# Shared expert with its weights stationary: gate and up products turned, inner values written to PSUM

## Chip, cores and metric

The kernel runs on one core of a Trainium2 chip. The metric is device time of one execution in microseconds, the lower the better; several executions give a median.

## What is computed

Sixteen sequences of 128 tokens with 256 features pass through a pre-norm decoder layer: causal attention with 16 heads and rotary positions, a long convolution gated by a context tensor, and a feed-forward part with 16 routed experts (4 per token) and one shared expert. The change touches the shared expert alone:

```python
x = x + attn(layernorm(x)); x = x + conv_mix(layernorm(x), ctx)
h = layernorm(x)                                   # 2048 tokens x 256
gate, up = split(h @ shared_gate_up.T, 704)        # shared_gate_up: 1408 x 256
shared = (silu(gate) * up) @ shared_down.T         # 704 -> 256
shared = shared * sigmoid(h @ shared_gate_vec.T)
out = x + shared + sum_of_routed_experts(h)
```

Products are made of fp16 pairs: every fp32 operand is a high and a low half, and a product is high x high, high x low and low x high, three matmuls. Silu is computed with a tanh: silu(g) = g/2 (1 + tanh(g/2)).

## The kernel before, in words

Work runs in two phases. In the first, one *row* (one sequence of 128 tokens) enters per *stage*, and the pieces of several rows are interleaved; in the second, 79 tiles of 128 sorted tokens pass through the routed experts. Each engine has a list of pieces (`ORDER`), written out by hand, which it goes through once per stage; `name:behind` means that in stage s the piece works on row s - behind. Every engine runs its list strictly in order and waits at semaphores. Stages 0 to 4 fill the pipeline, stages 5 to 16 hold every piece, and a second written list (`DRAIN`) finishes rows 12 to 15 and what is left of the others. Names of pieces that the text uses:

- TensorE: `px` prefix sums for routing (lines 689 to 694); `ga0`, `ga1`, `up0`, `up1` gate and up of the shared expert, each for 352 of the 704 inner values (`half_product`, line 705); `v` and `qk` projections (528); `sc01`, `sc23` scores (568, 574); `pt0` to `pt3` transposes of probabilities (585); `at0` to `at3` attention times values (597); `cv0` to `cv3` quarters of the convolution (632, 636); `Th0`, `Th1` transposes of the inner values (`turn_shared`, 715); `t5` transpose for the feed-forward (660); `dn` the shared down product (727); `Tq`, `Tk` transposes of query and key terms (558).
- ScalarE: `th0`, `th1` tanh of the gates (1003); `hh0`, `hh1` high halves of the transposed inner values (1011); `ex0` to `ex3` exponentials (942, four instructions each); `ph0` to `ph3` copies of transposed probabilities (954); `kh2` the high half of a convolution operand (972); `cq`, `ck` copies of the transposed terms (923).
- VectorE: `s10`, `s11` (1 + tanh) x gate (1310); `s20`, `s21` times up, which gives the inner values (1320); `hl0`, `hl1` low halves (1327); `mx0` to `mx3` row maxima (1150); `pw` and `ky` routing steps (1285, 1295); `nr3` a normalisation shift (1113); `gm0` to `gm3` gating of the convolution (1206).
- GpSimd: `kl0` to `kl3` low halves of the convolution operands (1577).

Apart from these pieces ScalarE and VectorE also split the weights into halves, one *unit* after another as it is loaded. Where the units come in is set by the tables `PREPARE` (ScalarE) and `PREPARE_LO` (VectorE): `(stage, n): (units)` puts them ahead of the n-th piece of the list in that stage. VectorE's half of a unit is line 1347 or 1343.

PSUM has eight banks. `PSUM_ORDER` lists for each bank which pieces use it, in turn; before a piece writes, `free` waits until the reader of the use before has finished (table `READER`). In the kernel before, bank 0 is used by `up0`, `cv0`, `xT` (which `t5` writes) and `o2T` in turn, and `up0` counts as read when `s20` is done:

```python
"up0": (inner_done, 1), "up1": (inner_done, 2), "ih0": (inner_lo, 1), "ih1": (inner_lo, 2),
```

The operands of the convolution live in two buffers: `kh2` may only write when `cv0` has run, `kl2` follows `kh2`, and `cv2` needs `kl2`.

The shared expert of one row: tokens are the stationary operand and 352 weight columns move, so tokens lie on partitions; the inner values are computed in SBUF, transposed by TensorE (`Th0`, `Th1`) into PSUM, split into halves and multiplied by the down weights.

Of the kernel before, what the change touches and what calls it, by code (L numbers as in the profile page):

```python
# [1751 lines left out]
```

## Time and profile before

| what | us |
|---|---|
| median of three runs (608.62 to 612.01) | 611.7 |
| the profiled execution's own time | 609.71 |
| span of that execution in the profile | 607.9 |
| TensorE busy in the span | 575.1 (95%) |
| VectorE, ScalarE, GpSimd busy | 479.1, 413.0, 387.7 |

The span runs from the first to the last instruction of the profile; the execution's own time is 1.8 us longer. A busy TensorE counts matmuls from start to modelled end; matmuls overlap, so the time that one costs is read from the distance between starts.

### The profile page before, as it was taken

Reading aid. Unit: us, or ns where it says so; the run is one execution under the profiler, and the core shown is the slowest. Engines: PE = TensorE matmul, PEld = TensorE weight load, DVE = VectorE, ACT = ScalarE, POOL = GpSimd, SP = SyncE. Lnnn points to the kernel's source line nnn. Section 1 sums busy time; section 2 is a strip of 40 time slices with the busy share of each in tenths; the row PEclk is TensorE's granted clock in tenths of the full one; section 3 lists DMA queues with packets and bytes.
Section 4 is the critical chain, followed back from the end, with each engine's and each line's share of the span. In section 5 each row is a group of like instructions: output and inputs, shape, how many; then the busy total and the mean of one; then the engine's idle time right before and its main releaser. Section 6 shows DMA issues by size and latency. Waiting matters only on the chain.

```text
span 607.9 us, 18533 instructions
## 1 busy us (share of the span) xinstructions
PE 575.1 (95%) x5887; PEld 466.1 (77%) x5887; DVE 479.1 (79%) x1454; ACT 413.0 (68%) x1060; POOL 387.7 (64%) x419
## 2 busy tenths in 40 slices
PE   8889899999999999999999999998899999999991
PEld 3558679888898898888888889876677777777770
DVE  4657788878878688798877776687688899999993
ACT  4876876878768778787686775832266666666661
...
GB/s 227 295 80 174 92 111 122 80 132 116 92 135 79 114 115 62 148 83 129 90 87 86 14 87 24 32 45 63 146 128 135 175 222 237 235 238 233 243 179 112
DMA packets 55681, 78.99 MB, mean 130 GB/s; under 512 B 7202, under 2 KB 46370, under 8 KB 55588
## 3 DMA queue, kind: packets, MB, share of 16 engines
...
q8 instruction: 52, 0.85, 0.6%
...
HBM read 44.48 MB, written 33.29 MB: 128 GB/s over the span
## 4 chain that ended last, share of the span: by engine, by line
PE 78%; issue 7%; POOL 6%; DVE 4%; ACT 3%; DMA 1%; POOLq 0%; DVEq 0%; ACTq 0%
PE ps L832 12%; PE ps L705 9%; PE ps L597 7%; PE ps L632 6%; PE ps L528 5%; PE ps L727 5%; PE ps L855 4%; PE ps L652 3%; PE ps L585 3%; PE ps L636 3%; PE ps L844 3%; PE ps L821 3%; POOL kv_lo L1577 2%; PE ps L568 2%; PE ps L558 2%
## 5 line engine op out<-in xcount | busy, mean ns | idle before, releaser
L1577 POOL TENSOR_TENSOR kv_lo<-kv,kv_hi 128x512 f16<-128x512 f32 x64 | 80.9, 1265 | 30.2 <-ACT kv_hi L972 29.5
L1643 POOL DMA_INDIRECT toeplitz_lo<-y_slots,slots x44 | 42.5, 965 | 81.0 <-DMA y_slots<-kv 61.6
L832 PE MATMUL ps<-w_gate_up_hi,toeplitz_hi 128*128 x316 | 84.0, 314 | 1.4 <-DVE toeplitz_hi L1482 1.1
L1565 POOL TENSOR_TENSOR kv<-ctx_t_sb,v_t 128x512 f32<-128x512 f32 x60 | 64.9, 1090 | 16.0 <-ACT v_t L962 15.9
L1609 POOL DMA_INDIRECT x_slots<-x_norm,slots x60 | 65.0, 1084 | 15.1 <-issue 14.3
L942 ACT ACTIVATE probs<-ps,row_neg_max 128x128 f32<-128x128 f32 x256 | 71.5, 391 | 0.3 <-DVE row_neg_max L1150 0.3
L597 PEld LDWEIGHTS ps<-v_ones,probs_t 128*128 128x128 f32 x512 | 62.2, 192 | 2.2
L597 PE MATMUL ps<-v_ones,probs_t 128*128 128x17 f32 x512 | 60.7, 256 | 0.0
L1537 POOL TENSOR_TENSOR ln_rstd<-ln_var,minus_half 128x1 f32<-128x1 f32 x48 | 30.3, 632 | 43.1 <-DVE ln_var L1105 43.1
L632 PE MATMUL ps<-kv_hi,toeplitz_hi 128*128 128x128 f16 x256 | 56.7, 221 | 1.3 <-POOL kv_lo L1577 0.7
L632 PE MATMUL ps<-kv_hi,toeplitz_lo 128*128 128x128 f16 x256 | 56.6, 221 | 0.0
L1059 ACT ACTIVATE toeplitz_hi<-ps 128x256 f16<-128x256 f32 x79 | 30.2, 383 | 38.8 <-ACT stage L1078 17.4
L632 PE MATMUL ps<-kv_lo,toeplitz_hi 128*128 128x128 f16 x256 | 56.5, 221 | 0.0
L1206 DVE TENSOR_TENSOR conv_gated<-ps,ctx_t_sb 128x512 f32<-128x512 f32 x64 | 43.6, 684 | 12.4 <-PE ps L636 12.2
L636 PE MATMUL ps<-kv_lo,toeplitz_hi 128*128 128x64 f16 x256 | 49.7, 194 | 0.0
L636 PE MATMUL ps<-kv_hi,toeplitz_lo 128*128 128x64 f16 x256 | 49.7, 194 | 0.0
L636 PE MATMUL ps<-kv_hi,toeplitz_hi 128*128 128x64 f16 x256 | 49.7, 194 | 0.0
L832 PE MATMUL ps<-w_gate_up_lo,toeplitz_hi 128*128 x158 | 49.4, 313 | 0.0
L1150 DVE TENSOR_REDUCE row_neg_max<-ps 128x4 f32<-128x512 f32 x64 | 43.3, 682 | 7.6 <-PE ps L574 7.6
L972 ACT ACTIVATE kv_hi<-kv 128x512 f16<-128x512 f32 x64 | 40.1, 627 | 9.5 <-PE ps L636 8.5
L954 ACT ACTIVATE probs_t<-ps 128x512 f32<-128x512 f32 x64 | 38.7, 609 | 11.3 <-PE ps L585 10.7
L832 PEld LDWEIGHTS ps<-w_gate_up_hi,toeplitz_hi 128*128 128x128 f16 x316 | 30.7, 97 | 19.8 <-issue 9.4
...
## 6 DMA issues: line engine op xcount, KB each, us to landing
...
```

The source lines that it names most:

```text
L597: last = nc.tensor.matmul(bank("av")[:, h * (HD + 1):(h + 1) * (HD + 1)], pT[g % 2][:, s, :], v_sb[row % 2][:, h, :], start=True, stop=Tru ...
L632: nc.tensor.matmul(to, toep_w[a][:, QUADS * g + h, 0, :], kvh[b][g % 2][:, h, :, :].rearrange("p c n -> p (c n)"), start=first, stop=end, ...
L636: last = nc.tensor.matmul(to[:, 64:128], toep_w[a][:, QUADS * g + h, 1, :], kvh[b][g % 2][:, h, 0, :], start=first, stop=end, skip_group_c ...
L705: last = nc.tensor.matmul(bank(use, row)[:, 0:CH], xT[a][row % 2][:, kc, :], sgu[b][:, c, kc, side, :], start=first, stop=end)
L832: last = nc.tensor.matmul(psum[2 + t % 2][:, 0:2 * INTER], bxT[a][t % 2][:, kc, :], egu[b][:, bass.ds(e, 1), kc, :].rearrange("p a n -> p ...
L942: last = nc.scalar.activation(sm[g % 2][:, s, :], bank(f"sc{g}")[:, s * P:(s + 1) * P], ACT.Exp, bias=mx[row % 2][:, g, s:s + 1])
L1150: nc.vector.tensor_reduce(mx[row % 2][:, g, :], bank(f"sc{g}")[:].rearrange("p (s n) -> p s n", n=P), X, ALU.max, negate=True).then_inc(ma ...
L1206: nc.vector.tensor_tensor(to, y, cT.broadcast_to([P, QUADS, KC, SIDE, SIDE]), ALU.mult)\
L1565: nc.gpsimd.tensor_tensor(kv[g % 2][:], cs.broadcast_to([P, SIDE, SIDE, SIDE]), vs.broadcast_to([P, SIDE, SIDE, SIDE]), ALU.mult).then_inc ...
L1577: nc.gpsimd.tensor_tensor(flat(kvh[1][g % 2]), kv[g % 2][:].rearrange("p h j i -> p (h j i)"), flat(kvh[0][g % 2]), ALU.subtract).then_inc ...
L1609: pool.indirect_dma_start(out=xbuf, out_offset=bass.IndirectOffsetOnAxis(ap=slots[:, row, j:j + 1], axis=0), in_=xn3_of(row), in_offset=No ...
L1643: pool.indirect_dma_start(out=yg[n][j], out_offset=None, in_=ybuf[0:(last_tile(row, j) + 1) * P], in_offset=bass.IndirectOffsetOnAxis(ap=s ...
```

## The change

Gate and up change sides: 128 columns of weights are now stationary and the 128 tokens move, so that inner values come out on partitions and no transpose is needed. The 1408 columns are ordered as 384 gate, 384 up, 256 gate, 320 up and 64 gate, in 11 chunks of 128; the last chunk of `up1` holds 64 columns of up and 64 of gate, for which two pieces are new, `t1b` on ScalarE (a tanh of 64 x 128) and `s1b` on VectorE. `Th0`, `Th1` and the buffers `inner0`, `inner1` are gone: `s20` writes its product to the PSUM bank `ih0` and `s21` writes over `up1`, and `hh`, `hl` read them there. The shared gate's weight per token, which `s20` and `s21` applied, moves to the piece that adds the result to x. Banks are dealt anew, `pt1` stands ahead of `cv0` on TensorE, and `s20` stands behind `nr3` on VectorE. The tables of the weight units keep their stages and are renumbered.

```diff
 PSUM_ORDER = (
-    "up0:5 cv0:3 xT:4 o2T:3",
+    "up0:5 cv0:3 cv2:3 o2T:3",
...
-    "up1:5 cv2:3 xnT:0",
+    "up1:5 xnT:0",
...
-    "px:5 pt1:2 ih1:5 oT:2 wo:2",
+    "px:5 pt1:2 xT:4 oT:2 wo:2",
     "sc1:2 ih0:5 ro:4 tq:1",
...
-            "up1": (inner_done, 2), "ih0": (inner_lo, 1), "ih1": (inner_lo, 2), "dn": (xsh_ready, 1),
+            "up1": (inner_lo, 2), "ih0": (inner_lo, 1), "dn": (xsh_ready, 1),
...
-PREPARE_LO = {(2,9): (2,), (2,15): (3,), (2,30): (4,), (2,40): (5,), (3,30): (6,7), (3,42): (8,),
+PREPARE_LO = {(2,9): (2,), (2,15): (3,), (2,29): (4,), (2,41): (5,), (3,29): (6,7,), (3,43): (8,), (3,45): (9,),
...
-            def half_product(c, side, use, ready):
+            def half_product(use, first_col, chunks, ready):
...
-                    for kc in range(KC):
-                        for a, b, first, end in products(kc == 0, kc == KC - 1):
-                            last = nc.tensor.matmul(bank(use, row)[:, 0:CH], xT[a][row % 2][:, kc, :],
-                                                    sgu[b][:, c, kc, side, :], start=first, stop=end)
+                    for n in range(chunks):
+                        cols = slice(first_col + n * P, first_col + (n + 1) * P)
+                        for kc in range(KC):
+                            for a, b, first, end in products(kc == 0, kc == KC - 1):
+                                last = nc.tensor.matmul(bank(use, row)[:, n * P:(n + 1) * P], sgu[b][:, kc, cols],
+                                                        xT[a][row % 2][:, kc, :], start=first, stop=end,
+                                                        skip_group_check=True)
                     last.then_inc(ready.sem, 1)
-            def turn_shared(c):
...
+            pieces |= {"ga0": half_product("ga0", 0, 3, gate_ready), "up0": half_product("up0", 3 * P, 3, up_ready),
+                       "ga1": half_product("ga1", 6 * P, 2, gate_ready), "up1": half_product("up1", 8 * P, 3, up_ready)}
...
             def shared_up(c):
                 def piece(row):
-                    gate_done.wait(dve, row, c + 1)
+                    gate_done.wait(dve, row, 1 + 2 * c)
                     up_ready.wait(dve, row, c + 1)
-                    cws_done.wait(dve, row)
-                    inner_T.wait(dve, row - 1, c + 1)
-                    nc.vector.scalar_tensor_tensor(out=hh[c][:, 0:CH], in0=bank(f"up{c}", row)[:, 0:CH], scalar=cws[row % 2][:],
-                                                   in1=th[c][:], op0=ALU.mult, op1=ALU.mult).then_inc(inner_done.sem, 1)
+                    if c == 0:
+                        free(dve, "ih0", row)
+                    nc.vector.scalar_tensor_tensor(out=bank(("ih0", "up1")[c], row)[:, 0:CHP], in0=bank(f"up{c}", row)[:, 0:CHP],
+                                                   scalar=SILU, in1=th[c][:], op0=ALU.mult, op1=ALU.mult)\
+                        .then_inc(inner_done.sem, 1)
```

On TensorE, in a full stage, before: from the first probability transposes `pt0` over `cv0` to the attention `at0`. The last word of a row is what it waits for; `inner_done` is given by `s20` and `s21`.

```order
L585 MATMUL ps<-identity,probs 128x128 [waits exped]
...
L632 MATMUL ps<-kv_hi,toeplitz_hi 128x128 [waits inner_done,kv_lo]
...
L715 MATMUL ps<-identity,inner 128x128 [waits exped,inner_done]
...
L585 MATMUL ps<-identity,probs 128x128 [waits page_step,exped]
...
L597 MATMUL ps<-v_ones,probs_t 128x17 [waits x_shared_ready,v_copied,probs_t_copied]
...
L632 MATMUL ps<-kv_hi,toeplitz_hi 128x128 [waits probs_t_copied,kv_lo]
...
L632 MATMUL ps<-kv_hi,toeplitz_hi 128x128 [waits inner_done,kv_lo]
```

The same place now; `pt1` is the row that waits for `page_step`.

```order
L589 MATMUL ps<-identity,probs 128x128 [waits exped]
L589 MATMUL ps<-identity,probs 128x128 x3
L589 MATMUL ps<-identity,probs 128x128 [waits page_step,exped]
L589 MATMUL ps<-identity,probs 128x128 x3
L636 MATMUL ps<-kv_hi,toeplitz_hi 128x128 [waits inner_done,kv_lo]
...
L601 MATMUL ps<-v_ones,probs_t 128x17 [waits x_shared_ready,v_copied,probs_t_copied]
...
L636 MATMUL ps<-kv_hi,toeplitz_hi 128x128 [waits probs_t_copied,kv_lo]
...
L636 MATMUL ps<-kv_hi,toeplitz_hi 128x128 [waits conv_gated,kv_lo]
```

Between `cv0` and `cv2` (the first and the last convolution row) there stood `Th0`, `pt1`, `at0` and `cv1`; now `pt1` stands ahead of `cv0`, and only `at0` and `cv1` are left between the two.

On VectorE, in stage 6, before: from the second row maximum `mx1` to `s21`. `inner0` is written by `s20`, `inner1` by `s21`, the unit of weights is line 1347.

```order
L1150 TENSOR_REDUCE row_neg_max1<-ps5 128x4
L1280 TENSOR_TENSOR slot_place<-ps4,slot_moved 128x16
L1320 SCALAR_TENSOR_TENSOR inner0<-ps0,shared_weight0,gate_th0 128x352
L1347 SCALAR_TENSOR_TENSOR w_gate_up_lo<-stage,w_gate_up_hi 128x704
L1285 SCALAR_TENSOR_TENSOR tile_fresh<-ps4,tile_newest0 128x16
L1150 TENSOR_REDUCE row_neg_max1<-ps7 128x4
L1295 SCALAR_TENSOR_TENSOR slot_key<-picked0,slot_place 128x16
L1099 BN_AGGR ln_mean_var0_1<-ln_stats0_1 128x2
L1113 TENSOR_SCALAR ln_shift2_1<-ln_mean_var2_1,ln_rstd2_1 128x1
L1320 SCALAR_TENSOR_TENSOR inner1<-ps2,shared_weight0,gate_th1 128x352
```

The same place now; `s20` writes bank 5 from bank 0.

```order
L1154 TENSOR_REDUCE row_neg_max1<-ps5 128x4
L1284 TENSOR_TENSOR slot_place<-ps4,slot_moved 128x16
L1361 SCALAR_TENSOR_TENSOR w_gate_up_lo<-stage,w_gate_up_hi 128x704
L1289 SCALAR_TENSOR_TENSOR tile_fresh<-ps4,tile_newest0 128x16
L1154 TENSOR_REDUCE row_neg_max1<-ps7 128x4
L1299 SCALAR_TENSOR_TENSOR slot_key<-picked0,slot_place 128x16
L1103 BN_AGGR ln_mean_var0_1<-ln_stats0_1 128x2
L1117 TENSOR_SCALAR ln_shift2_1<-ln_mean_var2_1,ln_rstd2_1 128x1
L1332 SCALAR_TENSOR_TENSOR ps5<-ps0,gate_th0 128x384
L1154 TENSOR_REDUCE row_neg_max1<-ps1 128x4
```

`s20` stood ahead of the unit and stands now behind it, behind a row maximum and behind three short steps. In stages 5, 6, 7, 8, 10, 12 and 13 a unit stands somewhere between `mx1` and `nr3`; in the other full stages there is none there.

## Rows read from the trace of the kernel before

**Rows 1.** Page, first line: span.

```profile
span 607.9 us, 18533 instructions
```

**Rows 2.** Windows, one full stage: us, busy us by engine, clock, DMA share, GB/s.

```profile
320.03:344.48 24.45, 24.45 (x290) 20.93 (x289) 18.24 (x59) 18.32 (x45) 20.08 (x22) 1.00 0.19 61
```

**Rows 3.** Timeline of TensorE in stage 15: start us, length us, instructions.

```profile
331.66 0.31 PE L705 MATMUL ps<-w_shared_gate_up_hi,moe_x_t_hi 128*128 128x352 f16 x1
...
332.56 0.27 PE L528 MATMUL ps<-w_attn_hi,lhs_t_hi 128*128 128x256 f16 x1
...
333.40 0.59 PE L568 MATMUL ps<-causal_bf,identity_bf 128*128 128x512 bf16 x2
...
336.92 0.60 PE L585 MATMUL ps<-identity,probs 128*128 128x128 f32 x4
337.35 0.22 PE L632 MATMUL ps<-kv_hi,toeplitz_hi 128*128 128x128 f16 x1
...
337.52 0.19 PE L636 MATMUL ps<-kv_hi,toeplitz_hi 128*128 128x64 f16 x1
...
338.37 0.53 PE L715 MATMUL ps<-identity,inner 128*128 128x128 f32 x3
338.74 0.60 PE L585 MATMUL ps<-identity,probs 128*128 128x128 f32 x4
...
339.98 0.22 PE L632 MATMUL ps<-kv_hi,toeplitz_hi 128*128 128x128 f16 x1
...
341.00 0.22 PE L632 MATMUL ps<-kv_hi,toeplitz_hi 128*128 128x128 f16 x1
...
342.71 0.49 PE L715 MATMUL ps<-identity,inner 128*128 128x128 f32 x3
343.04 0.96 PE L597 MATMUL ps<-v_ones,probs_t 128*128 128x17 f32 x8
```

**Rows 4.** Timeline of ScalarE in the same stage; in brackets idle time before and who ended it.

```profile
331.04 1.02 ACT L923 ACTIVATE q_terms_t<-ps 128x1024 f16<-128x1024 f16 x1 [1.28 <-PE ps L558]
...
332.22 1.03 ACT L923 ACTIVATE k_terms_t<-ps 128x1024 f16<-128x1024 f16 x1
...
335.26 2.16 ACT L942 ACTIVATE probs<-ps,row_neg_max 128x128 f32<-128x128 f32 x8
...
338.63 0.63 ACT L972 ACTIVATE kv_hi<-kv 128x512 f16<-128x512 f32 x1 [0.48 <-PE ps L636]
...
341.03 0.62 ACT L954 ACTIVATE probs_t<-ps 128x512 f32<-128x512 f32 x1
```

**Rows 5.** Timeline of GpSimd in the same stage.

```profile
339.34 1.15 POOL L1577 TENSOR_TENSOR kv_lo<-kv,kv_hi 128x512 f16<-128x512 f32 x1 [0.85 <-ACT kv_hi L972]
```

**Rows 6.** Timeline of VectorE in stage 6, and TensorE's `cv0` there.

```profile
114.76 0.58 DVE L1320 SCALAR_TENSOR_TENSOR inner<-ps,shared_weight,gate_th 128x352 f32<-128x352 f32 x1
115.25 1.57 DVE L1347 SCALAR_TENSOR_TENSOR w_gate_up_lo<-stage,w_gate_up_hi 128x704 f16<-128x704 f32 x1
...
116.82 0.68 DVE L1150 TENSOR_REDUCE row_neg_max<-ps 128x4 f32<-128x512 f32 x1
...
117.98 0.57 DVE L1320 SCALAR_TENSOR_TENSOR inner<-ps,shared_weight,gate_th 128x352 f32<-128x352 f32 x1
...
116.13 0.22 PE L632 MATMUL ps<-kv_hi,toeplitz_hi 128*128 128x128 f16 x1
```

**Rows 7.** Timeline of VectorE: the units at that place in stages 5, 12 and 13.

```profile
91.47 0.93 DVE L1347 SCALAR_TENSOR_TENSOR w_gate_up_lo<-stage,w_gate_up_hi 128x704 f16<-128x704 f32 x1
...
263.44 2.15 DVE L1347 SCALAR_TENSOR_TENSOR w_down_lo<-stage,w_down_hi 128x1024 f16<-128x1024 f32 x1
...
287.83 2.22 DVE L1343 SCALAR_TENSOR_TENSOR w_down_rest<-stage,w_down_rest 64x1024 f16<-64x1024 f32 x1
```

**Rows 8.** Stage 4: timeline of TensorE (`pt0`) and ScalarE (`ex0` and `ex1`).

```profile
67.90 0.63 PE L585 MATMUL ps<-identity,probs 128*128 128x128 f32 x4 [0.92 <-ACT probs L942]
...
66.61 2.17 ACT L942 ACTIVATE probs<-ps,row_neg_max 128x128 f32<-128x128 f32 x8
```

More of the change, by code:

```diff
@@ L23 @@
 CH = SHARED // 2
+MIX = SHARED - 5 * P
 CHP = 3 * P
@@ L104 @@
 DRAIN = {n: [(p.split(":")[0], int(p.split(":")[1])) for p in pieces.split()] for n, pieces in {
[21 rows of a table removed]
[23 rows of a table added]
 }.items()}
 LATE_BANKS = (
-    "cv0:14 xT:13 o2T:14 cv0:15 xT:14 o2T:15 xT:15 up0:15",
+    "o2T:14 cv0:15 xT:14 o2T:15 xT:15 up0:15",
     "cv3:14 vT:15 cv3:15",
-    "cv2:14 cv2:15 ro:14 px:14 ro:15 px:15 up1:15",
+    "up1:12 cv2:15 ro:14 px:14 ro:15 px:15 up1:15",
     "",
-    "wo:15 px:13 up1:13 ih1:13 up1:14 ih1:14 ih1:15",
+    "wo:15 px:13 up1:13 up1:14",
     "ih0:12 ro:13 up0:13 ih0:13 up0:14 ih0:14 ih0:15",
@@ L239, in build @@
         seen = sb("seen", [P, NB + 1, EXPERTS], F16)
-        th = [sb(f"gate_th{c}", [P, CH]) for c in range(2)]
-        hh = [sb(f"inner{c}", [P, CHP]) for c in range(2)]
+        th = [sb(f"gate_th{c}", [P, CHP]) for c in range(2)]
         hT = [[sb(f"inner_t{c}_{n}", [P, 3, P], F16) for n in ("hi", "lo")] for c in range(2)]
@@ L380, in free @@
                 u, r = LATE_AFTER[use, row]
-                READER[u][0].wait(pe, r, READER[u][1])
+                if (u, r) != ("up0", row):
+                    READER[u][0].wait(pe, r, READER[u][1])
                 return
@@ L406, in unit_of @@
             if u < U_SD:
-                c, kc = divmod(u - U_SGU, KC)
-                return sgu[half][:, c, kc].rearrange("p s n -> p (s n)"), 2 * CH
+                kc, part = divmod(u - U_SGU, 2)
+                return sgu[half][:, kc, part * SHARED:(part + 1) * SHARED], SHARED
             if u < U_GU:
@@ L702, in piece @@
                     free(pe, use, row)
-                    for kc in range(KC):
-                        for a, b, first, end in products(kc == 0, kc == KC - 1):
-                            last = nc.tensor.matmul(bank(use, row)[:, 0:CH], xT[a][row % 2][:, kc, :],
-                                                    sgu[b][:, c, kc, side, :], start=first, stop=end)
-                    last.then_inc(ready.sem, 1)
-                return piece
-            def turn_shared(c):
-                def piece(row):
-                    inner_done.wait(pe, row, c + 1)
-                    free(pe, f"ih{c}", row)
-                    for t in range(3):
-                        last = nc.tensor.transpose(bank(f"ih{c}")[:, t * P:(t + 1) * P], hh[c][:, t * P:(t + 1) * P],
-                                                   id_sb[:])
-                    last.then_inc(inner_T.sem, 1)
+                    for n in range(chunks):
[5 more added lines that the diff above has]
+                                                        skip_group_check=True)
+                    last.then_inc(ready.sem, 1)
                 return piece
@@ L737, in _ @@
                 pieces |= {f"pt{g}": t_probs(g), f"at{g}": attend(g), f"cv{g}": conv(g)}
-            for c in range(2):
-                pieces |= {f"ga{c}": half_product(c, 0, f"ga{c}", gate_ready),
-                           f"up{c}": half_product(c, 1, f"up{c}", up_ready), f"Th{c}": turn_shared(c)}
+            pieces |= {"ga0": half_product("ga0", 0, 3, gate_ready), "up0": half_product("up0", 3 * P, 3, up_ready),
+                       "ga1": half_product("ga1", 6 * P, 2, gate_ready), "up1": half_product("up1", 8 * P, 3, up_ready)}
             def count_pairs():
@@ L789, in _ @@
                 pieces[name](row)
-                if (name, row) in table_after:
-                    table_after[name, row]()
+                for piece in table_after.get((name, row), ()):
+                    piece()
             def emptied(b):
@@ L1002, in piece, with rest_tanh @@
                     inner_done.wait(act, row - 1, c + 1)
-                    nc.scalar.activation(th[c][:], bank(f"ga{c}")[:, 0:CH], ACT.Tanh, scale=0.5 / WS)\
+                    n = (3 - c) * P
+                    nc.scalar.activation(th[c][:, 0:n], bank(f"ga{c}")[:, 0:n], ACT.Tanh, scale=0.5 / WS)\
                         .then_inc(tanh_done.sem, 1)
                 return piece
+            def rest_tanh(row):
+                up_ready.wait(act, row, 2)
+                inner_done.wait(act, row - 1, 2)
+                nc.scalar.activation(th[1][MIX:P, 2 * P:CHP], bank("up1", row)[MIX:P, 2 * P:CHP], ACT.Tanh, scale=0.5 / WS)\
+                    .then_inc(tanh_done.sem, 1)
             def inner_split(c):
                 def piece(row):
-                    inner_T.wait(act, row, c + 1)
+                    inner_done.wait(act, row, c + 1)
                     down_done.wait(act, row - 1)
-                    nc.scalar.activation(hT[c][0][:].rearrange("p t n -> p (t n)"), bank(f"ih{c}")[:, 0:CHP], ACT.Copy)\
+                    nc.scalar.activation(hT[c][0][:].rearrange("p t n -> p (t n)"), bank(("ih0", "up1")[c], row)[:, 0:CHP], ACT.Copy)\
                         .then_inc(inner_hi.sem, 1)
@@ L1037, in _ @@
                 pieces |= {f"th{c}": shared_tanh(c), f"hh{c}": inner_split(c)}
+            pieces["t1b"] = rest_tanh
             for s in range(DRAIN_FROM):
@@ L1326, in piece @@
                     inner_hi.wait(dve, row, c + 1)
-                    nc.vector.tensor_tensor(hT[c][1][:].rearrange("p t n -> p (t n)"), bank(f"ih{c}")[:, 0:CHP],
+                    nc.vector.tensor_tensor(hT[c][1][:].rearrange("p t n -> p (t n)"), bank(("ih0", "up1")[c], row)[:, 0:CHP],
                                             hT[c][0][:].rearrange("p t n -> p (t n)"), ALU.subtract)\
@@ L1335, in shared_out @@
                     dve.wait_ge(s_xsh[row % 2], 16 * (row // 2))
-                nc.vector.scalar_tensor_tensor(out=xsh[row % 2][:], in0=bank("dn")[:, 0:E], scalar=1.0 / WS,
+                cws_done.wait(dve, row)
+                nc.vector.scalar_tensor_tensor(out=xsh[row % 2][:], in0=bank("dn")[:, 0:E], scalar=cws[row % 3][:],
                                                in1=x2_of(row), op0=ALU.mult, op1=ALU.add).then_inc(xsh_ready.sem, 1)
@@ L1410, in _ @@
                 pieces |= {f"s1{c}": shared_gate(c), f"s2{c}": shared_up(c), f"hl{c}": inner_split(c)}
+            pieces["s1b"] = rest_gate
             for s in range(DRAIN_FROM):
@@ L1709, in weight_units @@
     units += [toep[:, q:q + QUADS] for q in range(0, GROUPS, QUADS)]
-    sgu = a["L0_ffn_shared_gate_up"].reshape(2, 2, CH, KC, P).transpose(1, 3, 4, 0, 2)
-    units += [sgu[c, kc] for c in range(2) for kc in range(KC)]
-    down = a["L0_ffn_shared_down"].T.reshape(2, CH, E)
-    down = np.concatenate([down, np.zeros((2, CHP - CH, E), np.float32)], axis=1)
+    gate, up = np.split(a["L0_ffn_shared_gate_up"], 2, axis=0)
+    n, m = CHP, SHARED - MIX
+    sgu = np.concatenate([gate[:n], up[:n], gate[n:m], up[n:m], up[m:], gate[m:]], axis=0).reshape(2 * SHARED, KC, P)
+    units += [w[:, n:n + SHARED] for w in sgu.transpose(1, 2, 0) for n in (0, SHARED)]
+    down = a["L0_ffn_shared_down"].T
+    down = np.concatenate([down, np.zeros((2 * CHP - SHARED, E), np.float32)], axis=0)
     units += list(down.reshape(2, 3, P, E).transpose(0, 2, 1, 3))
```

30 lines of the change are left out of this document (18 added, 12 removed), and 75 rows, old and new, of tables (DRAIN, ORDER, PREPARE, PREPARE_LO).

## The prediction

> **What bounds the kernel now.** I read the page's first part, then the windows for single stages, then TensorE's timeline through one stage, and last the other engines' timelines at the places where TensorE takes something over from them. The profiled span is 607.9 us [rows 1]. In a full stage TensorE is busy for 24.45 of 24.45 us at a granted clock of 1.00 (the 2.4 GHz level), while VectorE, ScalarE and GpSimd have about 6, 6 and 4 us to spare [rows 2]. So a full stage is as long as TensorE's list plus what TensorE waits for, and work taken from TensorE pays only where nothing else is late there. There are twelve full stages (5 to 16), half of the span; the routed tiles that follow are not touched.
>
> **TensorE's own work, per row.** Removed: four half products; `ga1` starts at 331.66 and the next piece at 332.56 [rows 3], so 0.90 us each for 6 matmuls, 3.60 in all. Removed also: `Th0`, 338.37 to 338.74, and `Th1`, 342.71 to 343.04 [rows 3], 0.70 together. Added: 11 chunks x 6 = 66 matmuls of 128 columns, each with weights of its own. The nearest row is the convolution, fp16, 128x128 weights, new ones for each matmul: three of them from 337.35 to 337.52 [rows 3], 0.057 each, so 66 x 0.057 = 3.76. From below, 128 columns at the rate of 352 columns per 0.15 us would be 0.0545 (3.60); from above, the four fp32 transposes from 336.92 to 337.35 [rows 3] give 0.108 (7.1). I take 0.057, the same shape and type. The net is 3.76 - 3.60 - 0.70 = -0.54 us per row, -8.6 over 16 rows if all of it came through. By piece: `ga0`, `up0`, `up1` (18 matmuls, 1.03) grow by 0.13 each, `ga1` (12, 0.68) shrinks by 0.22.
>
> The Trainium skill, "TensorE: Matmul & The Clock Gate", section "Back-to-back issue gap", speaks against small matmuls: in a stream of weight loads and matmuls it gives about 81 ns per matmul of 128 columns. The trace differs, with 57 ns for such pairs [rows 3]. By the Trainium skill's figure 66 matmuls would be an estimated 5.35 us, and each row 1.05 longer instead of 0.54 shorter.
>
> **What eats the saving in a plain stage.** Four waits, with each one's fixed length from the trace.
>
> (a) `sc01` starts at 333.40 [rows 3], after ScalarE's copies of the transposed terms: the first begins at 331.04, released by TensorE, and the second ends at 333.25 [rows 4]. That chain does not change, and `ga1` lies beside it. TensorE comes 0.22 earlier and waits 0.22 longer: gain nil. From here I count from `sc01`.
>
> (b) `up0` and `up1` push `pt0` from 336.92 to 337.18; `pt1`, which now stands ahead of `cv0`, takes another 0.43 (as long as `pt0` [rows 3]) and ends at 338.04. Its exponentials end at 337.42 [rows 4], so it does not wait. `cv0` needs `s20`, which now waits for the same exponentials (bank `ih0` follows `sc1`) and takes 0.58 x 384/352 = 0.63 [rows 6]: done at 338.05. The write to PSUM instead of SBUF is not shown by any row; I take 0, bounded by -0.1 and +0.3. So `cv0` starts at 338.05 to 338.1, a wait of at most 0.05, and ends at 339.1.
>
> (c) From the end of `cv0` (338.37, where `Th0` starts [rows 3]) `kh2` follows at 338.63 [rows 4] and `kl2` ends at 340.49 [rows 5]: 2.12, so about 2.15 until `cv2` can start. Between them stood 341.00 - 338.37 = 2.63 us of TensorE work; with `Th0` gone and `pt1` ahead of `cv0`, `at0` (0.81) and `cv1` (1.02) are left [rows 3], 1.83. TensorE waits 0.32. Behind `cv2` queue all later pieces of the stage.
>
> (d) `t5` now takes the bank of `pt1` and needs `ph1`, which ends at 341.03 + 0.62 [rows 4], 3.28 after the end of `cv0`; TensorE gets there after 2.15 + 1.02 = 3.17: 0.1.
>
> From `sc01` to the end of `pt3` that is +0.26 - 0.70 + 0.05 + 0.32 + 0.1 = +0.03, and `ga0` adds 0.13 later, ahead of nothing that could absorb it. A plain stage becomes 0.16 longer, x 12 = +1.9. The new `t1b` and `s1b` lie in spare time: ScalarE is idle 0.48 ahead of `kh2` [rows 4], VectorE has the 6 us of [rows 2].
>
> **What costs most: `s20` behind the weight units.** Both lists of VectorE are in the section on the change. In stages 5, 6, 7, 8, 10, 12 and 13 a unit's low half stands between `mx1` and `nr3`. It used to stand behind `s20`; now `s20` is behind it, and `cv0` waits for `s20`. In stage 6 `s20` started at 114.76, the unit at 115.25, `s21` at 117.98 [rows 6], so unit to `s21` is 2.73. The unit now starts at 114.76 and `s20` takes the place of `s21`: 117.49, done at 118.12. TensorE is ready for `cv0` at 116.13 [rows 6] plus 0.26 + 0.43 = 116.82. It waits about 1.3 us, and nothing later in the stage gives this back, since (c) and (d) run from the end of `cv0`, and (a) from the next `Tq`. For stages 7, 8 and 10, whose units have the same shape, I take the same. Stage 5 has a unit of 0.93 in place of 1.57 [rows 6, 7]: 0.7. Stages 12 and 13 have 2.15 and 2.22 [rows 7]: 1.9 each. Sum: 0.7 + 4 x 1.3 + 2 x 1.9 = +9.7. The low end is near 5, if units take 0.93 everywhere (0.7 x 5 + about 0.7 x 2); the high end 12, if the short steps behind the unit stretch too.
>
> **The filling and the draining.** In stages 3 and 4 there are no shared products between scores and `pt0`. In stage 4 `pt0` ran at 67.90, and `ex1` ends at 66.61 + 2.17 = 68.78 [rows 8]. `pt1` ahead of `cv0` therefore makes `cv0` start at 68.8 + 0.43 instead of 68.33, 0.9 later, and `kh2`, `kl2`, `cv2` follow. `pt1` no longer stands behind `cv0`, so I take 0.7 per stage (0 to 0.9), 1.4 for both. The drained rows 12 to 15 save at most 4 x 0.54 = 2.2; they get an extra VectorE step each where VectorE carries the routing chain. I take 0, with -2.2 and +2.
>
> **Sum.** +1.9 + 9.7 + 1.4 + 0 = +13.0. The profiled execution took 609.7, so 622.7; the runs shown (608.6 to 612.0, median 611.7) lie around 611, which gives 624.
>
> **Rivals.**
> 1. *TensorE's saving comes through* (faster). For it: TensorE is 100% busy in a full stage [rows 2]. Against it: (a) and (c) are chains whose length the change leaves, and the order of VectorE is as written. It needs `s20` on time in every stage and the waits (c) and (d) not there: 609.7 - 8.6 = 601 to 605.
> 2. *The two effects nearly cancel* (no change). The units run in about 0.9 us at their new place, so the stalls are near the low end of 5 us, and half of (c) is absorbed because ScalarE gets to `kh2` sooner (-2): 1.9 + 5 - 2 + 0.7 = +5.6, about 616. For it: stage 5 shows 0.93 [rows 7]. Against it: stage 6 shows 1.57 with GpSimd at work [rows 6].
> 3. *The new weights are not hidden* (much slower). Each matmul would step by more than 57 ns, at most by the 108 of the fp32 transposes: 66 x 0.051 = +3.4 us per row, +54, which with the stalls is above 660; a step of 0.08 gives 66 x 0.023 x 16 = +24, so 648. Against it: the convolution's 57 ns, and its 64-column matmuls go faster still (338.37 - 337.35 = 1.02 for 12 of each kind, so 0.028 each [rows 3]). The rule of the Trainium skill named above would be this rival.
>
> The three differ in sign at one point: how much later than TensorE `s20` is at `cv0`. With the plain stage as reckoned, an average stall of 0 gives about +3, 0.5 us in seven stages +7.
>
> **How the numbers follow.** Forecast 0.71, rival 1 0.11, rival 2 0.15, rival 3 0.03. About 1% is what a measurement of this kernel can tell from no change. Faster by over 1% (below 605.6): 0.11. Within 1%: rival 2 and the forecast's low edge, 0.17. Slower: 0.72. The forecast's own range is 618 to 630 (stalls of 5 to 12, PSUM write up to 0.3 in twelve stages, drain -2 to +2). The range for 8 in 10 must take in rival 2 and reaches down towards rival 1: 609 to 630.
>
> **What would show it.** Right: in stages 5 to 8, 10, 12 and 13 the first convolution matmul of `cv0` waits 0.7 to 2 us for VectorE's write of `ps`, and these stages last 25.3 to 26.6; the others last 24.6; `cv2` waits 0.3 for `kl2` in each; `sc01` waits 0.3; the new matmuls step by 0.057. Wrong: no wait at `cv0`, or stages of 24.0 us, would mean that VectorE is earlier than its order lets me think; a step over 0.06 would be rival 3; a longer tile phase would be a cause that I have not seen.

## The result and the profile after

The changed kernel takes 636.3 us (median of 6 executions, 631.7 to 639.8); the kernel before, run beside it, 610.9 (608.6 to 612.0). The ratio is 1.0425, 95% interval 1.0392 to 1.0458: slower, as forecast, but by 25 us where I had said 13, and above the range's end of 630. The profiled execution took 631.7 us, 22.0 more than that of the kernel before (609.7).

The page's first line and three windows of the changed kernel: stages 6, 12 and 15, as in [rows 2] (start and end; length; busy us of TensorE, its weight loads, VectorE, ScalarE, GpSimd; clock; DMA share; GB/s).

```profile
span 629.9 us, 19685 instructions
...
103.09:128.75 25.66, 24.92 (x328) 21.55 (x326) 20.41 (x61) 18.80 (x48) 20.45 (x22) 1.00 0.31 97
...
257.68:284.87 27.19, 24.93 (x325) 21.57 (x326) 22.70 (x63) 19.78 (x48) 19.91 (x22) 1.00 0.33 101
337.17:362.30 25.13, 24.84 (x328) 21.56 (x326) 19.79 (x60) 18.50 (x47) 20.17 (x22) 1.00 0.18 59
```

TensorE's list got shorter, but the plain stage 15 grew from 24.45 to 25.13 us: it now has 0.29 us of idle time, and its busy time grew as well (24.84). Stage 12 has 2.3 us of idle time. Stages are counted here from the start of one `qk` to the next; the *plain stage* is the length that the stages come back to where neither a weight unit nor the clock holds them up (stage 15 in the changed kernel). For every kernel of this study (the median of its executions; then us of the profiled execution, where "first `qk`" is that of stage 4 and "rest" is from the `qk` of stage 16 to the end of the span):

| kernel | median | first `qk` | plain stage | 12 full stages | rest |
|---|---|---|---|---|---|
| before | 610.9 | 75.3 | 24.45 | 293.5 | 239.1 |
| changed | 636.3 | 77.7 | 25.13 | 309.7 | 242.5 |
| e1_units | 622.1 | 77.6 | 25.13 | 301.9 | 241.1 |
| e2_rows | 632.9 | 77.4 | 24.87 | 311.4 | 241.7 |
| e3_pt1 | 632.0 | 76.1 | 25.13 | 309.8 | 242.3 |
| e4_before_pt1 | 618.2 | 79.2 | 24.55 | 297.8 | 240.5 |
| f1_three | 620.1 | 76.7 | 24.87 | 299.0 | 243.3 |
| f2p_psum | 623.7 | 78.4 | 24.88 | 300.3 | 246.0 |
| f2_sbuf | 613.4 | 78.4 | 24.39 | 292.9 | 244.6 |
| f3_all | 622.3 | 80.5 | 24.88 | 297.8 | 243.4 |
| f4_ph1 | 608.4 | 75.2 | 24.12 | 288.6 | 241.6 |
| f5_ck | 619.6 | 78.2 | 24.27 | 292.8 | 244.3 |
| b1_ck | 620.3 | 84.7 | 24.82 | 296.7 | 240.1 |
| b2_units | 609.0 | 74.0 | 24.45 | 292.4 | 240.6 |

The last three columns add up to the span of the profiled execution, which can lie some us from the median (`f2_sbuf`: 617.7 us where the median is 613.4). So the 22.0 us of the changed kernel are 2.4 in the filling, 16.2 in the twelve stages and 3.3 behind them. Of the 16.2, the plain stage's 0.68 x 12 is 8.2; the other 8.1 are stages longer than the plain one.

TensorE's waits (us in total, times, the longest):

```profile
PE ps L636 <- DVE ps L1332: 7.6, 7, 2.0
PE ps L589 <- ACT probs L938: 3.0, 6, 0.9
PE ps L664 <- ACT probs_t L950: 2.3, 13, 0.2
```

The first line is the forecast stall: `cv0` behind `s20`, in exactly seven stages, 7.6 us where I had 9.7; the kernel before has a single wait of that kind, of 0.2 us. The second line is `pt0` or `pt1` behind the exponentials (2.3 us in the kernel before). The third (`t5` behind `ph1`) is not in the list of the kernel before. The timeline of TensorE through stage 15, beside [rows 3]:

```profile
345.38 0.27 PE L724 MATMUL ps<-w_shared_down_hi,inner_t_lo 128*128 128x256 f16 x1
345.58 0.28 PE L724 MATMUL ps<-w_shared_down_hi,inner_t_hi 64*128 64x256 f16 x1
...
345.81 0.27 PE L724 MATMUL ps<-w_shared_down_hi,inner_t_lo 64*128 64x256 f16 x1
346.01 0.33 PE L652 MATMUL ps<-identity,skip_out 128*128 128x128 f32 x1
...
351.91 0.23 PE L711 MATMUL ps<-moe_x_t_hi,w_shared_gate_up_hi 128*128 128x128 f16 x1
351.97 0.22 PE L711 MATMUL ps<-moe_x_t_hi,w_shared_gate_up_lo 128*128 128x128 f16 x1
352.03 0.22 PE L711 MATMUL ps<-moe_x_t_lo,w_shared_gate_up_hi 128*128 128x128 f16 x1
...
354.80 1.04 PE L589 MATMUL ps<-identity,probs 128*128 128x128 f32 x8
355.76 0.22 PE L636 MATMUL ps<-kv_hi,toeplitz_hi 128*128 128x128 f16 x1
...
356.78 1.04 PE L601 MATMUL ps<-v_ones,probs_t 128*128 128x17 f32 x8
357.67 0.22 PE L636 MATMUL ps<-kv_hi,toeplitz_hi 128*128 128x128 f16 x1
...
358.66 0.19 PE L640 MATMUL ps<-kv_hi,toeplitz_lo 128*128 128x64 f16 x1
358.96 0.23 PE L636 MATMUL ps<-kv_hi,toeplitz_hi 128*128 128x128 f16 x1
...
359.96 0.19 PE L640 MATMUL ps<-kv_hi,toeplitz_lo 128*128 128x64 f16 x1
360.33 0.41 PE L664 MATMUL ps<-identity,x_norm 128*128 128x128 f32 x2 [0.18 <-ACT probs_t L950]
```

The new matmuls step by 0.06 and 0.055, as forecast. `cv2` starts 0.27 after `cv1` could hand over (358.66 + 0.03 to 358.96), `t5` 0.34 after `cv2`. And `dn` shows something that I had not counted: at its last chunk, whose weights have 64 rows, the step is 0.20 instead of 0.11, and again at the first matmul behind it.

What `cv2` and `t5` wait for, on ScalarE (`kh2`, `hh0`, `ph1`) and GpSimd (`kl2`), beside [rows 4, 5]:

```profile
357.04 0.63 ACT L968 ACTIVATE kv_hi<-kv 128x512 f16<-128x512 f32 x1 [0.70 <-PE ps L640]
...
359.20 0.50 ACT L1014 ACTIVATE inner_t_hi<-ps 128x384 f16<-128x384 f32 x1
359.57 0.62 ACT L950 ACTIVATE probs_t<-ps 128x512 f32<-128x512 f32 x1
```

```profile
357.75 1.16 POOL L1591 TENSOR_TENSOR kv_lo<-kv,kv_hi 128x512 f16<-128x512 f32 x1 [1.76 <-ACT kv_hi L968]
```

From the end of `cv0` (356.78) to `cv2` are 2.18 us; I had read 2.15 from the trace before.

VectorE in stages 6 and 12, unit and `s20`, beside [rows 6, 7]; then TensorE's `cv0` there:

```profile
119.56 0.88 DVE L1361 SCALAR_TENSOR_TENSOR w_gate_up_lo<-stage,w_gate_up_hi 128x704 f16<-128x704 f32 x1
...
121.51 0.55 DVE L1332 SCALAR_TENSOR_TENSOR ps<-ps,gate_th 128x384 f32<-128x384 f32 x1
...
275.44 2.15 DVE L1361 SCALAR_TENSOR_TENSOR w_down_lo<-stage,w_down_hi 128x1024 f16<-128x1024 f32 x1
...
277.64 0.55 DVE L1332 SCALAR_TENSOR_TENSOR ps<-ps,gate_th 128x384 f32<-128x384 f32 x1
```

```profile
122.21 0.22 PE L636 MATMUL ps<-kv_hi,toeplitz_hi 128*128 128x128 f16 x1 [0.45 <-DVE ps L1332]
...
278.33 0.22 PE L636 MATMUL ps<-kv_hi,toeplitz_hi 128*128 128x128 f16 x1 [1.97 <-DVE ps L1332]
```

The unit of stage 6 took 0.88 us at its new place, where 1.57 stood in [rows 6], and the stall is 0.45 where I had 1.3. Stage 12 came out as forecast (1.97 for 1.9).

Behind the stages, the chain of waits has its last `dn` at 453.96 in the changed kernel and at 435.33 in the kernel before (start, us):

```profile
453.96 3.56 PE ps L724 x18
```

```profile
435.33 2.14 PE ps L727 x18
```

From the last `qk` to there both took the same (66.54 and 66.56), so these two executions show no cost of the drain, as forecast. But TensorE's mean granted clock in that stretch was 1.00 in the changed kernel and 0.97 in the kernel before, so part of the equality is the clock's.

At the last `dn` itself it was the other way round. TensorE waited 1.0 to 1.1 us just ahead of it in both, and its mean granted clock over `dn` was 1.00 in the kernel before and 0.59 in the changed one, mostly the 1.2 GHz level; the window around it there:

```profile
453.00:458.00 5.00, 4.04 (x20) 2.38 (x21) 1.88 (x6) 0.00 (x0) 0.00 (x0) 0.66 0.39 110
```

So this `dn` took 1.4 us longer (about 0.2 of it are the 64 rows of the next section). The other 1.9 of the 3.3 lie in the routed tiles, which the change does not touch; their cause is open.

### The profile page after: what moved, and what is told of

Its sections match the earlier page's. It is cut to its first block, busy times and chain, and to the rows that moved or that the text cites. A ratio compares the mean times of both kernels' runs of the same rounds, so it can differ in the third digit from the quotient of the medians.

```text
span 629.9 us, 19685 instructions
## 1 busy us (share of the span) xinstructions
PE 579.9 (92%) x6463; PEld 476.2 (76%) x6463; DVE 493.4 (78%) x1468; ACT 416.5 (66%) x1076; POOL 387.3 (61%) x419
## 4 chain that ended last, share of the span: by engine, by line
PE 68%; issue 10%; ACT 7%; DVE 7%; POOL 4%; DMA 2%; POOLq 0%; ACTq 0%; DVEq 0%
PE ps L828 11%; PE ps L711 7%; PE ps L532 6%; PE ps L724 5%; PE ps L601 5%; PE ps L636 4%; PE ps L851 4%; PE ps L656 3%; PE ps L589 3%; PE ps L840 3%; ACT probs L938 2%; PE ps L817 2%; PE ps L640 2%; PE ps L572 2%; PE ps L562 2%
## 5 line engine op out<-in xcount | busy, mean ns | idle before, releaser
L1591 POOL TENSOR_TENSOR kv_lo<-kv,kv_hi 128x512 f16<-128x512 f32 x64 | 77.5, 1213 | 47.2 <-ACT kv_hi L968 47.1
L1579 POOL TENSOR_TENSOR kv<-ctx_t_sb,v_t 128x512 f32<-128x512 f32 x60 | 68.9, 1157 | 18.9 <-ACT v_t L958 18.8
L711 PE MATMUL ps<-moe_x_t_hi,w_shared_gate_up_hi 128*128 128x128 f16 x352 | 62.2, 220 | 2.1 <-DVE inner_t_lo L1340 2.1
L601 PE MATMUL ps<-v_ones,probs_t 128*128 128x17 f32 x512 | 62.2, 259 | 0.0
L711 PE MATMUL ps<-moe_x_t_lo,w_shared_gate_up_hi 128*128 128x128 f16 x352 | 62.0, 219 | 0.0
L711 PE MATMUL ps<-moe_x_t_hi,w_shared_gate_up_lo 128*128 128x128 f16 x352 | 62.0, 219 | 0.0
```

The costliest lines, as they stand in the source:

```text
L601: last = nc.tensor.matmul(bank("av")[:, h * (HD + 1):(h + 1) * (HD + 1)], pT[g % 2][:, s, :], v_sb[row % 2][:, h, :], start=True, stop=Tru ...
L711: last = nc.tensor.matmul(bank(use, row)[:, n * P:(n + 1) * P], sgu[b][:, kc, cols], xT[a][row % 2][:, kc, :], start=first, stop=end, skip ...
L1579: nc.gpsimd.tensor_tensor(kv[g % 2][:], cs.broadcast_to([P, SIDE, SIDE, SIDE]), vs.broadcast_to([P, SIDE, SIDE, SIDE]), ALU.mult).then_inc ...
L1591: nc.gpsimd.tensor_tensor(flat(kvh[1][g % 2]), kv[g % 2][:].rearrange("p h j i -> p (h j i)"), flat(kvh[0][g % 2]), ALU.subtract).then_inc ...
```

## The experiments

The diffs are shortened to the entries and lines that matter; "the changed kernel" is the one that the forecast was for.

**e1_units: the stalls of `cv0` alone.**

```diff
-(5,29): (14,) (6,27): (16,) (7,27): (18,) (8,27): (21,) (10,28): (25,) (12,31): (29,) (13,29): (32,)
+(5,34): (14,) (6,34): (16,) (7,34): (18,) (8,34): (21,) (10,34): (25,) (12,34): (29,) (13,34): (32,)
```

> The changed kernel with one edit: in stages 5, 6, 7, 8, 10, 12 and 13 the weight unit's low half that VectorE made ahead of s20 is made behind mx3, ahead of gm0. Theory 1 (the seven waits of cv0 for s20, 7.6 us in the trace, come from these units alone): the waits are gone, stages 6 to 13 last 25.1 to 25.4 us instead of 25.5 to 27.4, and the time falls by 6 to 8 us, to about 625 in the profiled execution. Rival (VectorE has too much to do in these stages, wherever the unit stands): gm0 then comes late, cv2 waits for its bank instead of cv0 for s20, and at most 3 us come back.

Measured: 622.1 us, ratio to before 1.0179 (1.0144 to 1.0215). The wait for `s20` is gone from the list, and the same two stages, 6 and 12, in its windows:

```profile
101.32:126.45 25.13, 24.84 (x327) 21.54 (x325) 20.57 (x61) 18.81 (x48) 19.86 (x22) 1.00 0.30 100
253.78:278.93 25.15, 24.86 (x326) 21.57 (x327) 21.53 (x63) 19.79 (x48) 19.93 (x22) 1.00 0.35 108
```

The twelve stages lose 7.8 us and the profiled execution 9.3, theory 1. Stages 9 and 11, which have units elsewhere in VectorE's list, are still long (25.65 and 25.99 us), outside the 25.1 to 25.4 of the text. The medians fall by 14, more than the waits were. The changed kernel's six executions run from 631.7 us at a mean granted clock of 0.988 to 639.8 at 0.972; those of e1_units from 621.0 to 622.9 at 0.986 to 0.992. So the stalls seem to cost clock as well; the next run's trace shows it in one execution.

**e2_rows: the 64 weight rows.**

```diff
-n = MIX if (c, t) == (1, 2) else P
+n = P
```

> The changed kernel with one edit: the last chunk of dn reads 128 rows instead of 64 (the added rows meet weights that are zero). Theory 2 (a change of the number of weight rows from 128 to 64 and back costs TensorE about 0.1 to 0.2 us each time): dn falls from 2.12 to about 1.9 us and the time by 0.2 to 0.25 us per row, 3 to 4 us over 16 rows. Rival (the time is that of dn's place, beside other work): dn stays at 2.1 and the time does not move by more than 1 us.

Measured: 632.9 us, 3.4 less, and 24.87 instead of 25.13 per plain stage: theory 2, 0.26 per row. The reading rests on the plain stage, since the executions of the two kernels overlap (630.2 to 633.6 and 631.7 to 639.8). The start of the last chunk of `dn` and the end of `dn` there:

```profile
322.36 0.27 PE L724 MATMUL ps<-w_shared_down_hi,inner_t_lo 128*128 128x256 f16 x1
322.46 0.27 PE L724 MATMUL ps<-w_shared_down_hi,inner_t_hi 128*128 128x256 f16 x1
...
322.68 0.27 PE L724 MATMUL ps<-w_shared_down_hi,inner_t_lo 128*128 128x256 f16 x1
322.79 0.27 PE L652 MATMUL ps<-identity,skip_out 128*128 128x128 f32 x1
```

Both steps of 0.20 are gone. The kernel before had chunks of 96 rows, which cost nothing (18 matmuls in 1.97 us). The Trainium skill, "TensorEngine Tiling (Array Packing)", section "Tiling Modes", states that a change of tiling mode drains TensorE; a row tile of 64 is such a mode there and 96 is none. The rows agree in what costs and what does not, with 0.1 us more at each of the two changes; that it is a drain, no row here shows. The kernel before may show the same price: its scores have 48 weight rows, and from the two matmuls of 512 columns and 128 rows ahead of them (333.40 [rows 3]) to the first of 48 rows (333.92) are 0.52 us, where two such steps in `qk` take 0.43. No run changes that place.

In this execution two stages were long, 27.9 and 29.5 us. Their windows, around the two stalls of 1.97 us, which ended at 277.13 and 305.01:

```profile
276.00:277.40 1.40, 0.27 (x7) 0.30 (x8) 1.40 (x4) 0.00 (x0) 0.00 (x0) 1.00 0.05 9
...
279.00:281.00 2.00, 2.00 (x27) 2.00 (x27) 1.94 (x5) 1.98 (x8) 1.89 (x2) 0.51 0.12 49
...
303.00:304.80 1.80, 0.05 (x1) 0.00 (x0) 1.77 (x6) 0.52 (x2) 1.17 (x1) 1.00 0.50 84
...
306.50:310.00 3.50, 3.50 (x38) 3.50 (x38) 2.69 (x7) 3.47 (x11) 3.00 (x4) 0.50 0.49 173
```

TensorE stood nearly idle in the first row of each pair; soon after its return, while it was fully busy, the granted clock was at 0.50, the 1.2 GHz level. The two stages are 1.0 and 2.6 us longer than those of the changed kernel less 0.26. The same stalls in the changed kernel's profiled execution left the clock at 1.00 in stage 12 (window above). So a stall of 2 us was followed, in this execution, by a further loss of half its length in one stage and 1.3 times its length in the next. That this is what made the other executions of the changed kernel 2 to 8 us longer than the profiled one is argued from their mean clocks, not seen in a trace of them.

**e3_pt1 and e4_before_pt1: the place of `pt1`.** In the changed kernel back behind `cv0`; in the kernel before ahead of it.

```diff
-pt0:2 pt1:2 cv0:3 at0:2
+pt0:2 cv0:3 pt1:2 at0:2
```

> The changed kernel with one edit: pt1 stands behind cv0 again in TensorE's list. Theory 3 (in a plain stage s20 holds cv0, so the cover that cv2 gets back is paid at cv0): cv0 waits 0.3 to 0.4 us for s20 in every stage, cv2 waits no more, plain stages stay within 0.1 of 25.13; the filling gives back 1.4 to 2.4; in sum 1 to 3 us less. Rival (pt1's place alone makes the waits of cv2 and t5): each plain stage is 0.4 to 0.6 shorter, and the time falls by 5 to 8 us.

```diff
-pt0:2 cv0:3 Th0:5 pt1:2 at0:2
+pt0:2 pt1:2 cv0:3 Th0:5 at0:2
```

> The kernel before with one edit: pt1 stands ahead of cv0 in TensorE's list. Theory 3 (with Th0 still there, 2.20 us of work cover the 2.18 from the end of cv0 to cv2): full stages stay at 24.45 to 24.55, the filling gets 1.4 to 2.4 us longer, in sum 1 to 3 us more than before. Rival (the place of pt1 is what lengthens the plain stages): 0.4 or more per stage, 5 us or more in sum.

e3_pt1: the plain stage stays at 25.13, and the wait is now at `cv0`:

```profile
354.20 0.22 PE L636 MATMUL ps<-kv_hi,toeplitz_hi 128*128 128x128 f16 x1 [0.36 <-DVE ps L1332]
```

The filling gives back 1.6. Theory 3: `s20` is what holds the stage, and the place of `pt1` only decides where TensorE waits for it. The time, 632.0 (628.5 to 636.5), fell by more than the 1 to 3 us of the text, but the twelve stages are unchanged (309.8 for 309.7).

e4_before_pt1 fell between the two: 618.2 us, 8 more than before, which is the rival's sum, not theory 3's 1 to 3. Plain stages are 24.55, as theory 3 had it, and the filling 3.9 longer instead of 1.4 to 2.4. But stages 6, 7 and 8 last 25.4 (and 9 and 11 25.3, which I did not trace). TensorE in stage 7 of this kernel, then VectorE:

```profile
145.15 0.60 PE L585 MATMUL ps<-identity,probs 128*128 128x128 f32 x4
146.50 0.63 PE L585 MATMUL ps<-identity,probs 128*128 128x128 f32 x4 [0.75 <-DVE tile_fresh L1285]
```

```profile
144.70 1.57 DVE L1347 SCALAR_TENSOR_TENSOR w_gate_up_lo<-stage,w_gate_up_hi 128x704 f16<-128x704 f32 x1
146.19 0.16 DVE L1285 SCALAR_TENSOR_TENSOR tile_fresh<-ps,tile_newest 128x16 f32<-128x16 f32 x1
```

`pt1` takes the bank that `pw` (`tile_fresh`) has read, and `pw` stands behind the unit. Neither theory had that bank. It is one reason why moving `pt1` forward is not free for the kernel before either; what lengthens the filling I did not trace.

**f1_three: the three edits together.** e1_units, e2_rows and e3_pt1.

> The changed kernel with the three edits of the first runs together: the seven weight units behind mx3, dn's last chunk with 128 rows, pt1 behind cv0. Theory (the three costs lie one behind the other on TensorE and add up): plain stages 24.87 us as with the 128 rows alone, stages 5 to 13 without stalls, first qk near 76.1; in sum 9 + 4 + 1.5 us less than the changed kernel's 631.7, about 617. Rival (they overlap): 620 or more.

Measured: 620.1 us (profiled 620.7), plain stage 24.87, twelve stages 299.0. In the stages the costs add up (-7.8 and 12 x -0.26 make -10.9; -10.7 measured). The sum of 617 was missed by 3.7, of which 2.1 are behind the last `qk`, compared with e1_units.

**f2p_psum and f2_sbuf: what makes `s20` late.** Both put `s20` ahead of `pw`; f2_sbuf also writes the inner values to SBUF.

```diff
-mx1:2 pp:5 pw:5 mx2:2 ky:5 ag1:0 nr3:4 s20:5 mx3:2
+mx1:2 pp:5 s20:5 pw:5 mx2:2 ky:5 ag1:0 nr3:4 mx3:2
```

> As the run with three edits, and s20 stands ahead of pw and mx2 in VectorE's list, as in the kernel before, still writing to PSUM. Theory (bank ih0 behind sc1 holds s20 until ex1 has ended, so its place in the list gives nothing): VectorE waits for ScalarE's exponentials at s20, cv0 still waits about 0.3, plain stages stay at 24.8 to 24.9, the time at that of the run with three edits. Rival (the place in the list held it): 24.4 to 24.5 per plain stage, 5 us less.

f2_sbuf, on top of it:

```diff
-free(dve, "ih0", row)
+inner_lo.wait(dve, row - 1, 1)
-out=bank(("ih0", "up1")[c], row)[:, 0:CHP]
+out=inner(c, row)
-"sc1:2 ih0:5 ro:4 tq:1"
+"sc1:2 ro:4 tq:1"
+hh = sb("inner0", [P, CHP])
+def inner(c, row): return bank("up1", row)[:, 0:CHP] if c else hh[:]
```

> As the run before it in this call, and s20 writes its inner values to a buffer in SBUF instead of bank ih0; the split reads them there. Theory (the bank, not VectorE's write, made s20 late): cv0 waits no more, cv2 stays covered by pt1, at0 and cv1 (2.26 for 2.18), plain stages 24.4 to 24.5, 4 to 5 us less than with PSUM, about 612. Rival (something else holds cv0 or cv2): 24.8 per plain stage and no gain.

f2p_psum: 24.88 per plain stage, nothing gained, and VectorE's timeline shows why; below it ScalarE's `ex0` and `ex1`:

```profile
346.61 0.57 DVE L1332 SCALAR_TENSOR_TENSOR ps<-ps,gate_th 128x384 f32<-128x384 f32 x1 [1.33 <-PE ps L711]
```

```profile
344.31 2.18 ACT L938 ACTIVATE probs<-ps,row_neg_max 128x128 f32<-128x128 f32 x8
```

VectorE stands still for 1.33 us. The bracket names TensorE, which had long delivered `up0`; `ex1` ends at 344.31 + 2.18 = 346.49, and `s20` starts right after. f2_sbuf: 24.39 per plain stage, 613.4 us, ratio 1.0043 (1.0021 to 1.0066). So with `s20` ahead of `pw`, the bank behind `sc1` costs 0.49 us per stage. The place in the list counts as well: in f1_three, where `s20` stands behind `nr3`, VectorE has no idle time ahead of it, and it starts at the same point of the stage as in f2p_psum (17.62 us after `qk` in both). Bank and place hold it equally late there, and only the two edits together set it free; SBUF at the late place was not run. The write itself costs nothing: 0.55 to 0.57 us to PSUM, 0.55 to SBUF.

**f3_all, f4_ph1, f5_ck: the remaining waits.** f3_all changes three things on top of f2_sbuf; f4_ph1 leaves `ck` and `vT` in their old order; f5_ck exchanges them after all, with another bank for `vT`.

```diff
-hh0:6 ph1:3 ex3:3
+ph1:3 hh0:6 ex3:3
-(9,38): (23,24,) (11,38): (27,28,)
+(9,41): (23,24,) (11,41): (27,28,)
-cq:2 vT:3 ck:2
+cq:2 ck:2 vT:3
```

> As the run with SBUF, and on ScalarE ck stands ahead of vT, ph1 ahead of hh0; the units of stages 9 and 11 stand behind gm1. Theory (sc01 waits 0.24 for ck and t5 0.2 to 0.3 for ph1 in each stage): both waits go, plain stages 23.9 to 24.1, stages 9 and 11 0.3 to 0.8 shorter, about 606, below the kernel before. Rival (TensorE then waits as long at the next of these chains, ex1, ph0 or cv2): 24.3 to 24.5, and no more than 1 us less than with SBUF alone.

```diff
-cq:2 ck:2 vT:3
+cq:2 vT:3 ck:2
```

> As the run with SBUF (s20 to a buffer in SBUF, ahead of pw; pt1 behind cv0; dn with 128 rows; units behind mx3), with ph1 ahead of hh0 on ScalarE and the units of stages 9 and 11 behind gm1, but ck and vT in their old order. Theory (the slower time of the run that also exchanged ck and vT came from v alone, which waits for vT's bank): t5 starts 0.2 earlier, plain stages 24.15 to 24.25, stages 9 and 11 as the others; 3 to 4 us less than with SBUF alone, about 610, level with the kernel before. Rival (the next chain takes the 0.2): 24.35 to 24.4, 1.3 us less.

```diff
-cq:2 vT:3 ck:2
+cq:2 ck:2 vT:3
-"v:2 sc3:2 pt3:2 cv3:3 vT:2"
+"v:2 sc3:2 pt3:2 cv3:3"
-"av:2 dn:5"
+"av:2 dn:5 vT:2"
```

> As the run before it, and vT gets a place in the bank of av and dn, so that ck can stand ahead of vT on ScalarE without v waiting for it. Theory (sc01 waits 0.15 to 0.25 for ck in each stage): that wait goes, plain stages 23.95 to 24.05, about 2 us less, 608, a little below the kernel before. Rival (vT's later copy makes kv0, kh0 and ex0 late by as much): no change, 24.2.

f3_all: 622.3 us and 24.88 per plain stage, outside both texts. `v` takes the bank that `vT` leaves, so the exchange put the wait there (14 times, 13.6 us); TensorE's first matmul of `v`:

```profile
341.83 0.27 PE L536 MATMUL ps<-w_attn_hi,lhs_t_hi 128*128 128x256 f16 x1 [0.90 <-ACT v_t L962]
```

f4_ph1: 608.4 us, ratio to before 0.9981 (0.9966 to 0.9996), the theory. One of its plain stages:

```profile
315.25:339.37 24.12, 24.12 (x328) 21.56 (x326) 19.60 (x60) 18.43 (x47) 20.45 (x22) 1.00 0.19 63
```

TensorE is busy throughout, for 0.33 us less than in [rows 2] and 0.27 less than in f2_sbuf, and stages 9 and 11 are as short as the plain ones. f5_ck: 619.6 us, worse than its rival had it: 24.27 per plain stage, up to 25.3 in others, and 3.1 more ahead of the first `qk`. GpSimd's products need `vT`, and its waits for it grow from 15.6 to 29.8 us.

**b1_ck and b2_units: the same edits on the kernel before.** b1_ck is the last diff on it, b2_units has the units of stages 9, 11 and 13 and `ph1` moved, without the turned product.

> The kernel before with that last edit alone (vT in the bank of av and dn, ck ahead of vT). Theory (there sc01 waits at most 0.08 for ck, so the chain does not bound it): 24.35 to 24.45 per stage, at most 1 us less than before. Rival (the chain bounds the kernel before as well): 24.2 or less, 3 us.

> The kernel before with the edits of the best version that have nothing to do with the turned product: the units of stages 9 and 11 behind gm1, that of stage 13 ahead of gm0, ph1 ahead of hh0. It asks whether the best version owes its time to the turned product. Theory (its plain stages of 24.12 against 24.45 come from the product, these edits only clear stages 9, 11 and 13 of 0.31, 0.31 and 0.54): plain stages stay at 24.45, about 1.1 us less than before, 608.6. Rival (the edits carry it): plain stages fall to 24.3 or less, 606 or less.

b1_ck: 620.3 us, 24.82 per stage and 9.4 us more ahead of the first `qk`: neither text; the exchange hurts there as well, and `pt0` waits 0.16 for its exponentials. b2_units: 609.0 us, ratio 0.9989 (0.9968 to 1.0009), plain stages 24.45, twelve stages 1.1 shorter, as its theory had it. So the turned product, with its faults mended, gives f4_ph1 its 0.33 per plain stage, and 3.8 us over the twelve. In the whole time it is within the measurement of b2_units. In the profiled executions f4_ph1 gives 1.2 us back ahead of the first `qk` (75.2 for 74.0) and 1.4 between the last `qk` and the last `dn` (68.04 for 66.65 in b2_units and 66.56 in the kernel before). Two windows there, f4_ph1 and the kernel before:

```profile
389.00:396.50 7.50, 6.89 (x66) 6.30 (x66) 3.47 (x13) 1.63 (x6) 3.76 (x4) 0.58 0.10 36
```

```profile
395.00:401.00 6.00, 5.38 (x58) 3.92 (x57) 3.85 (x16) 1.11 (x5) 3.86 (x5) 0.72 0.14 48
```

The clock is lower for longer in f4_ph1. Why is open.

## Why the prediction was right in sign and half the size

The sum missed the profiled execution by 9.0 us (13.0 for 22.0): 6.2 too little for the plain stages, 1.6 too much for the stalls, 1.0 too little for the filling, and 3.3 behind the stages where it had nothing. The median lies another 3.4 higher.

- *Step of the new matmuls, 0.057*: right, 0.055 to 0.06. Rival 3 fell. The figure of about 81 ns in the Trainium skill, "TensorE: Matmul & The Clock Gate", section "Back-to-back issue gap", does not hold for this stream.
- *`s20` behind the units, +9.7*: the mechanism was right, shown by e1_units; 7.6 us of wait, 7.8 in the stages. The sizes of single stages were off. In stages 6, 7, 8 and 10 the unit took 0.88 us, as rival 2 had supposed, and the stalls are 0.45 to 0.53 instead of 1.3: at its new place the unit starts ahead of GpSimd's product and no longer behind it (last section); in stage 5 it is 1.75 instead of 0.7; in 12 and 13 1.97 for 1.9.
- *The plain stage, +0.16*: this is the step that failed, +0.68 measured, 6.2 us more over twelve stages. Term by term in stage 15: `up0` and `up1` +0.22 (0.26 forecast); `ga0` +0.10 (0.13); the transposes away, -0.70; `cv0` +0.10 (0.05); `cv2` +0.27 (0.32); `sc01` nil, as forecast; `t5` +0.34 (0.1); `at0` 0.89 instead of 0.81, +0.08 (nothing), and 0.82 again in e3_pt1, where `pt1` stands ahead of it; `dn` and the matmul behind it +0.25 (nothing). Sum +0.66. So the missed terms are `dn`, which I had read as unchanged because its number of matmuls is, and `t5`: `ph1` ended 3.41 after `cv0` instead of 3.28, and I had left out that TensorE starts 0.14 after the end of its row (360.33 for 359.57 + 0.62). Two runs show these two: e2_rows gives back 0.26 for `dn`, and f4_ph1, with `ph1` ahead of `hh0`, is 0.27 below f2_sbuf.
- *The cause behind (b) and (c)*: I had named `s20`'s new bank as a wait of at most 0.05, since `cv0` came just behind it. That hid its price. With `s20` late, `pt1` can fill the time ahead of `cv0` or that ahead of `cv2`, not both, and the stage is 25.13 either way (e3_pt1). With the bank away, `s20` early in the list and `pt1` behind `cv0`, the stage is 0.48 shorter than in f1_three (24.39 for 24.87).
- *The filling, +1.4*: 2.4; e3_pt1 gives back 1.6 of it. *The drain, nothing*: right up to the last `dn`, in part by luck, since the clock in the drain was higher than in the kernel before (1.00 for 0.97). The routed tiles added 1.9 us, which was in no term: it is what the prediction called a cause that it had not seen, and it stays open.
- *The clock*: left out of the sum. It adds about 1.2 us in the last `dn` of the profiled execution, and the median lies 4.6 us above that execution, 1.2 above for the kernel before.
- *Rival 1* (601 to 605) needed `s20` on time and the waits away. f4_ph1 has both, and its stages are 4.9 us shorter than before; the time is 608.4.
